# Three graph hops: 14 of the 782 chunks of edges gathered row by row from SyncE's queue, the rest by POOL into a ring of eight groups

## The reference, cut to what matters

```
def spmm(z):
    return segment_sum(edge_weight[:, None] * z[col], row, num_segments=N)
z = x
y = z @ weights[0]
for k in range(1, 4):
    z = spmm(z)
    y = y + z @ weights[k]
```

## Time and profile before

| | us |
|---|---|
| median of three runs | 9741.5 |
| lowest and highest | 9734.82, 9754.53 |
| the profiled execution | 9737.26 |
| its span, first to last instruction | 9735.5 |
| POOL's gathers of the first hop, first start to last start | 1169.8 to 2150.0 |
| of the second | 2172.3 to 3151.9 |
| of the third | 3185.0 to 4164.3 |

### The profile page before, as it was taken

The page is one execution under the profiler, slowest core; times in us unless marked ns, Lnnn a source line. Parts: engine busy times, 40 slices in busy tenths (PEclk is TensorE's granted clock), DMA queues, the critical chain, the costliest instruction groups (busy, mean ns, idle before and its releaser), DMA issues. The chain is left out here.

```text
span 9735.5 us, 171552 instructions
## 1 busy us (share of the span) xinstructions
PE 6374.2 (65%) x37681; PEld 5551.4 (57%) x37682; DVE 6539.5 (67%) x22695; ACT 2118.1 (22%) x6216; POOL 6993.0 (72%) x7418
## 2 busy tenths in 40 slices
PE   6777655547666577639404666767776688876666
PEld 5666544436655566634204666556675578766665
DVE  7555566668777777736305888877777666667777
ACT  5222100001111111112101222232222222223333
POOL 7777777767777777777776777547775577767775
PEclk7555555556666655569756888889999665667777
DMA  0000012122212212234303333222222322223333
GB/s 25 2 2 2 18 53 52 53 61 53 53 53 55 57 53 53 53 77 146 100 2 86 104 104 104 87 47 55 55 55 55 100 54 54 54 72 108 108 108 97
DMA packets 436037, 614.74 MB, mean 63 GB/s; under 512 B 176561, under 2 KB 312069, under 8 KB 435109
## 3 DMA queue, kind: packets, MB, share of 16 engines
q0 software_dynamic: 257024, 486.93, 19.6%
q1 hardware_dynamic: 178305, 119.49, 4.3%
q10 hardware_dynamic: 292, 3.41, 0.1%
HBM read 520.17 MB, written 89.19 MB: 63 GB/s over the span
## 5 line engine op out<-in xcount | busy, mean ns | idle before, releaser
L1179 PE MATMUL hop_sums<-hop_rows,hop_weighted 128*128 x4992 | 1152.1, 403 | 1053.2 <-SPq L1315 674.4
L1128 POOL DMA_INDIRECT hop_rows<-hops,k_src_gather x1568 | 1483.3, 946 | 486.8 <-issue 477.6
L1179 PEld LDWEIGHTS hop_sums<-hop_rows,hop_weighted 128*128 128x128 f32 x4992 | 989.6, 295 | 1158.8 <-issue 1158.7
L1505 POOL DMA_INDIRECT l_pass_rows<-left_table,k_dst_other x832 | 796.2, 957 | 433.2 <-issue 244.6
L1505 POOL DMA_INDIRECT l_pass_rows<-related,k_dst_typed x832 | 788.6, 948 | 308.6 <-issue 238.7
L1505 POOL DMA_INDIRECT l_pass_rows<-key_table,k_src_gather x784 | 744.3, 949 | 365.9 <-issue 234.8
L2000 POOL DMA_INDIRECT l_weigh_rows<-row_table,l_weigh_ring x832 | 790.0, 949 | 297.9 <-issue 213.1
L728 POOL DMA_INDIRECT src_sorted<-src_scatter_records,src_scatter_places x784 | 753.1, 961 | 260.4 <-issue 188.2
L1355 POOL DMA_INDIRECT dst_sorted<-rec,dst_places x768 | 752.8, 980 | 237.2 <-issue 237.2
L1128 POOL DMA_INDIRECT hop_rows<-in_x,k_src_gather x784 | 742.4, 947 | 249.0 <-issue 238.7
L1213 DVE TENSOR_SCALAR hop_weighted<-k_numbers,k_src_place,src_weight 128x128 f32<-128x128 f32 x2496 | 850.1, 403 | 15.7 <-issue 8.7
(11 more groups left out here) (477 smaller groups left out, 17048.9 us busy)
## 6 DMA issues: line engine op xcount, KB each, us to landing
related<-l_tables_rows SPq DMA_DIRECT2D x50, 1024.0 KB, 4.5
hop_rows<-hops,k_src_gather POOLq DMA_INDIRECT x1568
l_pass_rows<-related,k_dst_typed POOLq DMA_INDIRECT x832
l_pass_rows<-left_table,k_dst_other POOLq DMA_INDIRECT x832
l_weigh_rows<-row_table,l_weigh_ring POOLq DMA_INDIRECT x832
src_sorted<-src_scatter_records,src_scatter_places POOLq DMA_INDIRECT x784, 2.1
hop_rows<-in_x,k_src_gather POOLq DMA_INDIRECT x784, 2.5
dst_sorted<-rec,dst_places POOLq DMA_INDIRECT x784
```

Of the source, the lines that this page charges most:

```text
L1128: nc.gpsimd.indirect_dma_start(rows[:, s * G + g, :], None, table_in, bass.IndirectOffsetOnAxis(ap=o.gather[:, c:c + 1], axis=0),).then_in ...
L1179: last = nc.tensor.matmul(sums[:, b, g, :], weighted[:, s % SLOTS, g, :], rows[:, bass.ds(slots[g], 1), :], start=True, stop=True)
L1505: nc.gpsimd.indirect_dma_start(rows[:, s, g, :], None, table, bass.IndirectOffsetOnAxis(ap=index[:, c:c + 1], axis=0),).then_inc(got[s], 16)
```

## The change

The constants: 768 chunks (`MAIN`) stay with POOL, in a ring of 8 groups (`NEAR`) instead of 16. The last 16 places of the list (`SIDE`) get buffers of their own behind the ring; 14 of them hold edges (`BESIDE`), and the other two are zeroed on DVE in each hop. SP gathers the 14 x 128 = 1792 rows by one DMA each: behind each group's waits and increments it loads 10 node numbers (`BY_ROW`) into registers and issues 10 DMAs of one row of 512 bytes. That fills its groups 0 to 179 of 192 (the last of them with 2 rows). Seven semaphores count the rows, two columns each.

```
+NEAR = 8
+SIDE = 16
+MAIN = CU - SIDE
+BESIDE = CHUNKS - MAIN
+BY_ROW = -(-BESIDE * P // (MAIN // G - 4))
...
# hop, POOL
-            for n in range(GU):
-                s = n % RING
-                if n >= RING:
-                    pool.wait_ge(freed, n - RING + 1)
+            for n in range(MAIN // G):
+                s = n % NEAR
+                if n >= NEAR:
+                    pool.wait_ge(freed, n - NEAR + 1)
...
# hop, SP
-            for n in range(GU):
-                sp.wait_ge(got[n % RING], (n // RING + 1) * 16 * G)
+            order = [(p, c) for p in range(P) for c in range(BESIDE)]
+            for n in range(MAIN // G):
+                sp.wait_ge(got[n % NEAR], (n // NEAR + 1) * 16 * G)
                 sp.sem_inc(landed, 1)
-                if n >= RING // 2 and n + RING // 2 < GU:
+                if n >= NEAR // 2 and n + NEAR // 2 < MAIN // G:
...
                     sp.wait_ge(summed, reader)
                     sp.sem_inc(freed, 1)
+                mine = order[n * BY_ROW:(n + 1) * BY_ROW]
+                if mine:
+                    nodes = load_blocks(nc, sp.engine, o.side[:, n * BY_ROW:n * BY_ROW + len(mine)], len(mine), N - 1)
+                    for e, ((p, c), node) in enumerate(zip(mine, nodes)):
+                        sp.dma_start(rows[p:p + 1, NEAR * G + c, :], table_in[bass.ds(node, 1), :],
+                                     ).then_inc(side_got[(n * BY_ROW + e) // (2 * P)], 16)
+            for n in range(BESIDE // 2):
+                sp.wait_ge(side_got[n], 16 * 2 * P)
+            for n in range(SIDE // G):
+                sp.sem_inc(landed, 1)
...
# hop, DVE
+            nc.vector.memset(rows[:, NEAR * G + BESIDE:, :], 0.0)
...
# read_edges, SP: the table of nodes of the 14 chunks, turned into one row on one partition by way of DRAM
+        sp.wait_ge(listed, 2)
+        sp.dma_start(o.side_home, o.gather[:, MAIN:CHUNKS]).then_inc(side_in, 16)
+        sp.wait_ge(side_in, 16)
+        sp.dma_start(o.side[:], o.side_home.rearrange("(a p) c -> a (p c)", a=1)).then_inc(side_in, 16)
+        sp.wait_ge(side_in, 32)
...
# place_edges, DVE: the slot of a column in the new buffers
+        chain(nc.vector.tensor_single_scalar(aside[:], row_i[:], MAIN, ALU.is_ge))
+        chain(nc.vector.tensor_single_scalar(o.hop_slot, row_i[64:65, :], NEAR * G - 1, ALU.bitwise_and))
+        nc.vector.scalar_tensor_tensor(out=o.hop_slot, in0=aside[64:65, :], scalar=float(NEAR * G - MAIN % (NEAR * G)),
+                                       in1=o.hop_slot, op0=ALU.mult, op1=ALU.add)
```

More of the change, by code:

```diff
@@ L49 @@
 AFTER = NSLOT - E
+CHUNKS = -(-E // P)
+NEAR = 8
[3 more added lines that the diff above has]
+BY_ROW = -(-BESIDE * P // (MAIN // G - 4))
+assert 0 < BESIDE <= SIDE and MAIN % (NEAR * G) + SIDE <= NEAR * G
 assert TU * QU == CU and RING * G == 64 and NBLK < (RING - 2) * G
@@ L495, in place_edges @@
     block_f = sb("block_f", [P, CH])
-    row_i = sb("row_i", [1, CH], I32)
-    need_i = sb("need_i", [1, GROUPS], I32)
+    row_i = sb("row_i", [P, CH], I32)
+    aside = sb("aside", [P, CH], I32)
+    need_i = sb("need_i", [P, GROUPS], I32)
     starts = ps("starts", [HIS, 1])
@@ L566, in _ @@
         nc.vector.tensor_scalar(o.block_base[:], block_f[:], float(P), None, ALU.mult)
-        chain(nc.vector.tensor_copy(row_i[:], o.chunk[0:1, :]))
+        chain(nc.vector.tensor_copy(row_i[:], o.chunk[:]))
         chain(nc.vector.tensor_single_scalar(need_i[:], row_i[:, G - 1:CH:G], 2, ALU.arith_shift_right))
-        nc.vector.tensor_single_scalar(o.slot[:], row_i[:], RING * G - 1, ALU.bitwise_and)
-        nc.vector.tensor_scalar(o.need[:], need_i[:], 1.0, None, ALU.add)
+        nc.vector.tensor_single_scalar(o.slot[:], row_i[0:1, :], RING * G - 1, ALU.bitwise_and)
+        chain(nc.vector.tensor_single_scalar(aside[:], row_i[:], MAIN, ALU.is_ge))
+        chain(nc.vector.tensor_single_scalar(o.hop_slot, row_i[64:65, :], NEAR * G - 1, ALU.bitwise_and))
+        nc.vector.scalar_tensor_tensor(out=o.hop_slot, in0=aside[64:65, :], scalar=float(NEAR * G - MAIN % (NEAR * G)),
+                                       in1=o.hop_slot, op0=ALU.mult, op1=ALU.add)
+        nc.vector.tensor_scalar(o.need[:], need_i[0:1, :], 1.0, None, ALU.add)
         chain(nc.vector.tensor_single_scalar(block_f[:], block_f[:], float(NBLK - 1), ALU.min))
@@ L867, in read_edges @@
     limited = sem("limited")
+    side_in = sem("side_in")
     counted = sem("counted")
@@ L1020, in hop @@
         odd = k.x[:, 0:NBLK, :]
-        rows = sb("rows", [P, RING * G, D])
+        rows = sb("rows", [P, NEAR * G + SIDE, D])
         weighted = sb("weighted", [P, SLOTS, G, P])
         sums = ps("sums", [P, 2, G, D])
-        got = [sem(f"got{s}") for s in range(RING)]
+        got = [sem(f"got{s}") for s in range(NEAR)]
         landed = sem("landed")
@@ L1031, in hop @@
         freed = sem("freed")
+        side_got = [sem(f"side_got{n}") for n in range(BESIDE // 2)]
         running = sem("running")
@@ L1171, in a_round @@
                     n = i * DEEP + s
-                    slots = load_blocks(nc, pe.engine, o.slot[:, bass.ds(n * G, G)], G, RING * G - 1)
+                    slots = load_blocks(nc, pe.engine, o.hop_slot[:, bass.ds(n * G, G)], G, NEAR * G + SIDE - 1)
                     need = pe.value_load(o.need[:, bass.ds(n, 1)], min_val=1, max_val=GU)
@@ L1312, in _ @@
             home = table_out.rearrange("(b p) f -> p b f", p=P)
-            for n in range(GU):
-                sp.wait_ge(got[n % RING], (n // RING + 1) * 16 * G)
+            order = [(p, c) for p in range(P) for c in range(BESIDE)]
+            for n in range(MAIN // G):
+                sp.wait_ge(got[n % NEAR], (n // NEAR + 1) * 16 * G)
                 sp.sem_inc(landed, 1)
-                if n >= RING // 2 and n + RING // 2 < GU:
-                    reader = sp.value_load(o.free[:, n - RING // 2:n - RING // 2 + 1], min_val=SLOTS + 1, max_val=GROUPS + SLOTS)
+                if n >= NEAR // 2 and n + NEAR // 2 < MAIN // G:
+                    reader = sp.value_load(o.free[:, n - NEAR // 2:n - NEAR // 2 + 1], min_val=SLOTS + 1, max_val=GROUPS + SLOTS)
                     sp.wait_ge(summed, reader)
                     sp.sem_inc(freed, 1)
+                mine = order[n * BY_ROW:(n + 1) * BY_ROW]
[8 more added lines that the diff above has]
+                sp.sem_inc(landed, 1)
             for n, here in enumerate(pieces):
@@ L3156, in graph_network @@
             o.begins = sb(f"{n}_begins", [P, CH], BF16)
-            by_chunk = sb(f"{n}_by_chunk", [33, CH + SPARE], I32)
-            o.block, o.within = by_chunk[0:1, :], by_chunk[32:33, :]
+            by_chunk = sb(f"{n}_by_chunk", [65, CH + SPARE], I32)
+            o.block, o.within, o.hop_slot = by_chunk[0:1, :], by_chunk[32:33, :], by_chunk[64:65, 0:CH]
             o.sorted = dram(f"{n}_sorted", [LEAD + NSLOT + BEHIND, 4])
@@ L3164, in graph_network @@
         by_src.free = sb("src_free", [1, 2 * P], I32)
+        by_src.side_home = dram("src_side_home", [P, BESIDE], I32)
         by_dst.typed = sb("dst_typed", [P, CH + SPARE], I32)
@@ L3187, in graph_network @@
             by_src.chunk = sort.enter_context(nc.sbuf_tensor("src_chunk", [P, CH], F32))
+            by_src.side = sort.enter_context(nc.sbuf_tensor("src_side", [1, P * BESIDE], I32))
             with ExitStack() as unsorted:
```

## The result

| | before | after |
|---|---|---|
| median, us | 9741.5 | 10566.97 |
| lowest and highest | 9734.82, 9754.53 | 10561.8, 10577.23 |
| the profiled execution | 9737.26 | 10561.8 |
| its span | 9735.5 | 10560.1 |

The ratio is 1.0844 (95% interval 1.0829 to 1.0858): slower by 825 us. The forecast was 10,730, in a range of 10,200 to 11,060.

A forecast was written before the change was run, and what follows sets the result against it. POOL's gathers bound the kernel before; SP's queue would bound it after. Hops 970, tails 12 and 7, placing 2 sum to 991 us, on 9737.3 some 10,730 us, range 10,200 to 11,060.

The forecast's parts named there:

- The bound: In the hops: SP's in-order queue, 6.97 us a group against POOL's 5.0, becomes the bound; forecast's chance 0.83.
- the signs named ahead: Profile after: POOL waits some 320 us a hop, SP little; PE's wait grows like the hops; last eight groups 5.0 us.
- A row: SP's queue, each row DMA: 0.409 issue, 0.046 and 0.029 register instructions, three gaps of 0.035; 0.59 us.
- every issue behind another took 409 or more: SP's DMA issues: argument against the faster rival, that any issue right behind another took at least 409 ns.
- The load of ten: SP's register load of ten node numbers a group: 268 ns, 63 more and 35 for the gap, 0.37 us.
- 7 ns for each further one: Register loads: PE's 310 ns for one number and 332 for four, applied to SP's load of 10.
- The rival of 11,650: SP's register load is slow, 200 ns a number: 1.7 us more a group, kernel 11,650; chance 0.03.
- `landed` to `freed`: SP's existing work in each group, including a one-register load and the assertion behind it: stays 0.70 us.
- my rival of a faster kernel: SP's group takes less than 5.0 us, POOL stays the bound: 9698 us, if a row is below 0.406; chance 0.05.
- Tail and once-only costs: After the hops: 12 us first, 7 second, nothing third; once, 2.2 us for three DVE operations placing edges.
- the two DMAs ahead of the first hop: On SP, between gather table and meeting: two landings of 5.0 us, priced by a store called 100 times larger, fit in.
- the rival of 12,940: Rows back up in the DMA queue, one taking 1.0 us: SP's group 11.1 us, kernel 12,940; chance 0.07.

The follow-up runs named there:

- e1: The changed kernel with each group's ten node numbers at a stride of 12 instead of 10, so loads begin on 16-byte boundaries: 10247.12 us, ratio 1.053.
- e7: The changed kernel with SIDE = 12 alone: ten chunks by rows, seven rows a group, node numbers close together: 9818.2 us, ratio 1.0093 to the kernel before.
- e5: The changed kernel with SIDE = 12, ten chunks, seven rows a group, node numbers at a stride of 8: 9699.59 us, ratio 0.9962 to the kernel before.
- e2: The changed kernel without SP's row DMAs and their register loads, ring of eight kept: 9686.9 us, ratio 0.9953 to the kernel before.
- e6_probes: The changed kernel without rows and their register loads, plus two passes of register-load probes on SP ahead of the first hop: 9776.83 us in one run.

## Why the prediction was right, and where its sizes were off

**The bound: right, and shown.** That a gather is worth its time only as long as POOL sets the pace, and that the queue of SP takes over, is what the waits show; e1 and e7 move the time by moving SP's queue alone, and e5 hands the pace back to POOL. Of the signs named ahead, POOL's wait (325 us a hop for some 320), SP's (nearly none) and the last eight groups (5.0 us each) came; PE's wait for the landings grew by 458 us and not by about what the hops did.

**A row: mis-sized, 0.59 for 0.406 us.** I took a store's 409 ns as the issue because it came right behind another. What lengthened that one was not looked into; a row was 225 ns to issue, however many followed. That is 1.84 us a group too much. The register instructions (37 + 29 ns, the gaps) came as priced. The trace of the kernel before held shorter issues: ten loads to eight partitions each, one behind the other, in 3.42 us, and a store from 104 partitions in 0.30:

```profile
5183.68 0.30 SPq L770 DMA_DIRECT2D dst_breaks<-dst_read_breaks_sb  x1
5187.74 3.42 SPq L1479 DMA_DIRECT2D l_pass_brk<-dst_breaks  x10
```

That "every issue behind another took 409 or more" is so of the rows that the prediction cites, not of the trace; at the 0.30 of L1479 a row would have been an estimated 0.48, below the 0.49 at which the range was cut.

**The load of ten: mis-sized, 0.37 for 1.51 us.** The step that failed is "7 ns for each further one". It was read off one pair, one number and four on PE's queue, and carried on from four to ten. On SP's queue four numbers from a boundary cost 0.22 us and every number outside such a four 0.2. The Trainium skill (Runtime: NRT & Kernel Launch, section Instruction fetch mechanics) has some 200 ns for each register even in bulk, and I had set that aside. The trace agrees with it for the loads off a boundary (2.08 in the hops, 2.23 in the probe, for ten) and not for those on one, where four numbers come for the price of one. The rival of 11,650 had the load right for every second group (2.0 for 2.08), 0.5 too long in the mean, and the row wrong.

**`landed` to `freed`: 0.70 for 0.85.** The 0.70 is the difference of two times rounded to tenths; the mean in the trace before is 0.64. The rest is the load from `o.free`, which takes some 0.19 us more right behind rows, in the changed kernel as against its own groups without rows and as against e2. Why stays open: a load of one number took 462 ns in the first pass of e6_probes too, where nothing was in flight.

**The sum.** −1.84 + 1.14 + 0.15 + 0.26 of gaps is −0.29 us a group, 540 x 0.29 = 157 of the 163 us by which 10,730 lies above the median. The forecast was near because two errors of opposite sign met. It could have gone wrong the other way: my rival of a faster kernel was to decide "at a row of (5.13 - 1.07) / 10 = 0.406 us", and 0.406 us is just what a row takes. With rows priced right and the load left at 0.37 I should have called it even. With the load as measured, the rows had 0.24 us each (5.0 less 0.85, 1.51 and 0.26, by ten).

**Tail and once-only costs.** Between the hops 12 and 7 were forecast, 13.6 and 3.6 came. Behind the third hop came 3.8, where nothing was forecast; the 12 us of tail there fit the 11 by which DVE's wait at the meeting became shorter. The 2.2 us of the three operations of DVE are there, but the first `landed` is not later. Together 21.0 for 21, to the tenth by chance.

**What was hidden stayed hidden.** The ring of eight, the two DMAs ahead of the first hop and the zeroed buffers cost nothing that shows (e2, and the first `landed` at 1182.1). SP waited 1.1 and 1.4 us for the landings of the two DMAs; the store by which they were priced is 64 times as large as they are, not 100. The rows never backed up: an issue stayed at 224 to 320 ns over all 5376, so the rival of 12,940 has nothing for it.

## What to carry to other kernels

Work given to an engine whose queue is in order is priced as the sum of all that the queue then issues in a period, register loads included, against the period of the engine that it is to relieve. Over that line nearly the whole excess was lost here (6.68 and 5.26 us against 5.0), under it (4.76) the work cost nothing that shows. Price each instruction from a row of its own shape on its own queue, and look for the shortest such rows too: a DMA's issue by its shape, a register load by its count, where it begins and whether it comes right behind DMA issues. Node numbers that are loaded into registers were cheapest here in fours from a 16-byte boundary.

## What the runs showed of the hardware that I had not expected

- A register load on SP of 10 numbers takes longer (1128 ns) than one of 12 (915), and 8 bytes off a boundary it takes twice as long (2233).
- A register load right behind DMA issues takes some 0.19 us more than one behind another register load (462 for 268 ns for one number; 1.13 for 0.95 us for ten), also where those DMAs have landed. Why was not looked into.
- SP's issue of a DMA of 512 bytes takes 0.25 us for one piece on one partition and 0.42 for 16 pieces on 16 partitions. The number of partitions alone doesn't set it: a store from one took 409 ns, one from 104 took 301 (L770).
